# A four-layer vision state-space network in one kernel: layer 1's norms and gate in turns, the sampled convolution in halves, the projection with a bank per tile

## The reference

```python
# layer 0 (sampled convolution)
xz = einsum('bchw,ec->behw', x, in_proj_w); xin, z = split(xz, 2); z = silu(z)
t = gelu(batch_norm(conv3x3(xin, off1_w) + off1_b))
offset = tanh(conv1x1(t, off2_w)) * [1/(H-1), 1/(W-1)]
x_s = grid_sample_bilinear(xin, offset + ref)      # shifts of 0 to 1 point in y and x
# layer 1 (norm over channels, and a gate over the four directions)
xn = (x - mean_c(x)) * rsqrt(var_c(x) + 1e-5) * norm_g + norm_b
gate = softmax(tanh(xn @ gate_w1.T + gate_b1) @ gate_w2.T + gate_b2)
outs = mamba of xn in 4 directions;  y = sum_k gate[k] * outs[k]
```

## Time and profile before

| | us |
|---|---|
| median of 3 runs (lowest, highest) | 30857.21 (30854.06, 30863.32) |
| the profiled execution | 30855.04 |
| its span | 30853.3 |

### The profile page before, as it was taken

One profiled execution on the slowest core, in us unless ns is written; L12 is line 12 of the kernel. 1 busy time (PEld: TensorE's weight loads), 2 busy tenths in 40 slices (PEclk: granted clock), 3 DMA queues, 4 the chain that ended last, 5 costly groups with the idle time before them and its releaser, 6 DMA issues. The chain is left out here.

```text
span 30853.3 us, 332186 instructions
## 1 busy us (share of the span) xinstructions
PE 23829.2 (77%) x97030; PEld 7351.8 (24%) x97030; DVE 25538.5 (83%) x16489; ACT 14890.1 (48%) x20203; POOL 22839.6 (74%) x10221
## 2 busy tenths in 40 slices
PE   6877888888435688888886778888883778888885
PEld 3442222222112222222222422222221422222222
DVE  1259999999535999999993799999994689999995
ACT  1045555555134655555531555555551455555552
POOL 0028999999003699999992299999990189999991
PEclk8888888888756688888876888888886888888887
DMA  2042222221504422222235522222215532222224
GB/s 75 10 164 70 45 45 45 49 50 38 178 9 157 160 52 45 45 45 47 52 110 180 208 61 45 45 50 49 45 38 199 189 86 45 51 48 45 45 45 170
DMA packets 1155007, 2419.20 MB, mean 78 GB/s; under 512 B 118600, under 2 KB 656166, under 8 KB 1143680
## 3 DMA queue, kind: packets, MB, share of 16 engines
q1 hardware_dynamic: 1153224, 2397.86, 28.2%
HBM read 1374.43 MB, written 1023.05 MB: 78 GB/s over the span
## 5 line engine op out<-in xcount | busy, mean ns | idle before, releaser
L1355 POOL TENSOR_TENSOR scan_hc<-scan_bc,scan_h 128x1024 f32<-128x1024 f32 x6912 | 16086.7, 2362 | 108.3 <-DVE scan_h L1519 107.3
L1519 DVE TENSOR_TENSOR_SCAN scan_h<-scan_da,scan_state,scan_dbu 128x1024 f32<-128x1024 f32 x6912 | 15987.4, 2338 | 140.1 <-ACT scan_da L1407 133.9
L1438 PE MATMUL scan_da<-scan_dd,scan_ssel 32*128 32x512 f32 x27648 | 9101.0, 745 | 3013.1 <-DVE scan_h L1519 2781.0
L1407 ACT ACTIVATE scan_da<-scan_da,scan_a_cur 128x1024 f32<-128x1024 f32 x6912 | 7516.7, 1087 | 7720.6 <-PE scan_da L1438 7714.2
L1438 PE MATMUL scan_p_du<-scan_dd,scan_ssel 32*128 32x512 f32 x27648 | 9198.0, 745 | 534.2 <-DMA scan_bc<-bc_d 214.2
L1506 DVE TENSOR_TENSOR scan_dbu<-scan_p_du,scan_bc 128x1024 f32<-128x1024 f32 x4608 | 5561.0, 1207 | 506.1 <-PE scan_p_du L1438 475.5
L1341 POOL TENSOR_TENSOR scan_dbu<-scan_bc,scan_dus 128x1024 f32<-128x1024 f32 x2304 | 5446.0, 2364 | 145.7 <-ACT scan_dus L1381 145.1
L1438 PEld LDWEIGHTS scan_da<-scan_dd,scan_ssel 32*128 32x128 f32 x27648 | 2450.3, 216 | 10296.4 <-DVE scan_h L1519 8730.6
L1455 PE MATMUL scan_p_y<-scan_hc,scan_rsel 128*32 128x512 f32 x27648 | 4778.1, 772 | 17.2 <-POOL scan_hc L1355 16.8
L1438 PEld LDWEIGHTS scan_p_du<-scan_dd,scan_ssel 32*128 32x128 f32 x27648 | 2409.9, 211 | 3617.2 <-DVE scan_dbu L1506 2962.3
L1386 ACT ACTIVATE scan_state<-scan_h,scan_a_cur 128x1 f32<-128x1 f32 x6912 | 2025.1, 293 | 1584.3 <-DVE scan_h L1519 1476.4
(11 more groups left out here) (215 smaller groups left out, 14787.6 us busy)
## 6 DMA issues: line engine op xcount, KB each, us to landing
scan_bc<-bc_d SPq DMA_DIRECT2D x576, 512.0 KB, 12.1
du_d<-prep_useq SPq DMA_DIRECT2D x384, 576.0 KB, 3.8
delta_d<-prep_delta SPq DMA_DIRECT2D x384, 576.0 KB, 4.3
scan_dd<-delta_d SPq DMA_DIRECT2D x1152, 192.0 KB, 4.9
scan_dd<-du_d SPq DMA_DIRECT2D x1152, 192.0 KB, 6.7
y_d<-scan_y SPq DMA_DIRECT2D x576, 384.0 KB, 5.8
merge_y<-y_d SPq DMA_DIRECT2D x384, 576.0 KB, 5.8
xs_d<-proj_xs_o SPq DMA_DIRECT2D x96, 588.0 KB, 3.3
```

What stands on the lines that cost most here:

```text
L1355: nc.gpsimd.tensor_tensor(hc[:, u % HC_SLOTS, :], c, h[:, u % H_SLOTS, :], ALU.mult).then_inc(hc_ready, 1)
L1407: nc.scalar.activation(da[u % DELTA_BANKS][:], da[u % DELTA_BANKS][:], ACT.Exp, scale=a_cur[:, slot(u)[0], u % UNITS:u % UNITS + 1]).then_ ...
L1438: return nc.tensor.matmul(dst[:, half * H:(half + 1) * H], ssel[rows, i, :], dd[rows, s, m, j, :], start=True, stop=True)
L1519: nc.vector.tensor_tensor_scan(h[:, v % H_SLOTS, :], da[v % DELTA_BANKS][:], dbu[:, v % DBU_SLOTS, :], state[:, v % UNITS:v % UNITS + 1], ...
```

## The change

`norm_gate` is written in turns: turn t makes the first stage of step t, the second of step t-1 and so on up to the sixth turn behind, for both images at once. Mean and group scale are folded into one matmul with scaled centring weights (`scaled_c`); the variance is reduced to two rows, one an image, and the reciprocal of its root is spread back with gamma by a matmul; the hidden layers of both images lie in rows 0 to 31 and 32 to 63. Buffers are two or four deep.

`group_norm_head` waits for each half image on its own and loads the averaging weights last. `project` has eight banks, one a tile, copies and activates tile by tile, computes the third tile by two matmuls of 64 columns in place of two accumulating ones of 128, has its x (or `xn`) on 128 rows of which 32 are zeroed by POOL, and in layer 1 reads x in quarters with no copy. `conv_sampled` loads the grid in four bands, uses halves of 64 rows or 64 columns for the blocks that were half zero, and has offsets and spreads of earlier steps between the low part (tiles 0 and 1) and the high part (tile 2) of a step; the offset rows are kept twice, at rows 0 and 32, one for each axis. All loops are written out. Layouts of the weights follow.

The diff, cut (blank lines left out, indented less). `norm_gate`:

```diff
+    def centre_x(s):
+        t_.wait_ge(squared, s * IMAGES + ONE)
...
+        for b in range(IMAGES):
+            nc.tensor.matmul(p_c[:, b, 0:N], scaled_c[:, b, :], x[:, b, s * N:(s + 1) * N], start=True,
+                             stop=True).then_inc(centred, 1)
+    def square_sum(s):
+        t_.wait_ge(squared, (s + 1) * IMAGES + ONE)
+        t_.wait_ge(dev_ready, s + ONE)
+        for b in range(IMAGES):
+            last = nc.tensor.matmul(p_v[:, 0:N], mean[:, b, :], sq[:, s % 2, b, :], start=(b == 0), stop=(b == 1))
+        last.then_inc(var_done, 1)
...
+    def spread(s):
+        t_.wait_ge(inv_ready, s + 1 + ONE)
+        t_.wait_ge(scaled, s + ONE)
+        for b in range(IMAGES):
+            last = nc.tensor.matmul(p_r[:, b, 0:N], gamma[:, b, :], rs[:, s % 2, :], start=True, stop=True)
+        last.then_inc(scale_spread, 1)
+    def hide(s):
+        t_.wait_ge(xl_ready, s + 1 + ONE)
+        t_.wait_ge(tanh_ready, s + ONE)
+        for b in range(IMAGES):
+            q = HID_ROWS[b]
+            last = nc.tensor.matmul(p_hid[q:q + GATE_ROWS, 0:N], w1[:], xl[:, s % DEEP, b, :], start=True, stop=True)
+        last.then_inc(hidden, 1)
...
+    def make_logits(s):
+        t_.wait_ge(tanh_ready, s + 1 + ONE)
+        t_.wait_ge(soft, max((s - 1) * SOFT + 1, 0) + ONE)
+        for m in range(BLOCKS_T):
+            last = nc.tensor.matmul(p_log[:, m * IMAGES:(m + 1) * IMAGES, :].rearrange("p b k -> p (b k)"),
+                                    th[:, s % 2, m * P:(m + 1) * P], w2[:], start=True, stop=True)
+        last.then_inc(logits, 1)
...
+    def transpose(s):
+        t_.wait_ge(soft, (s + 1) * SOFT + ONE)
+        t_.wait_ge(gt_ready, s + ONE)
+        for m in range(BLOCKS_T):
+            last = nc.tensor.transpose(p_gt[:, m * P:(m + 1) * P],
+                                       lg[:, s % DEEP, m * IMAGES:(m + 1) * IMAGES, :].rearrange("p b k -> p (b k)"), eye[:])
+        last.then_inc(transposed, 1)
...
+    for t in range(TURNS):
+        if step(t):
+            centre_x(t)
+        if step(t - 1):
+            square_sum(t - 1)
+        if step(t - 2):
+            spread(t - 2)
+        if step(t - 3):
+            hide(t - 3)
+        if step(t - 4):
+            make_logits(t - 4)
+        if step(t - 6):
+            transpose(t - 6)
...
+    def deviation(s):
+        a.wait_ge(var_done, s + 1 + ONE)
+        a.wait_ge(inv_ready, s + ONE)
+        nc.scalar.activation(sd[:], p_v[:, 0:N], ACT.Sqrt, bias=eps[:]).then_inc(dev_ready, 1)
...
+    def square(s):
+        a.wait_ge(scaled, max(s - DEEP + 1, 0) + ONE)
+        a.wait_ge(var_done, max(s - 1, 0) + ONE)
+        for b in range(IMAGES):
+            a.wait_ge(centred, s * IMAGES + b + 1 + ONE)
+            nc.scalar.activation(xc[:, s % DEEP, b, :], p_c[:, b, 0:N], ACT.Identity, bias=shift[:, b:b + 1]).then_inc(xc_ready, 1)
+            nc.scalar.activation(sq[:, s % 2, b, :], p_c[:, b, 0:N], ACT.Square, bias=shift[:, b:b + 1]).then_inc(squared, 1)
...
+    def add_beta(s):
+        a.wait_ge(scaled, s + 1 + ONE)
+        a.wait_ge(xl_stored[s % DEEP], 16 * (s // DEEP) + ONE)
+        a.wait_ge(hidden, max(s - DEEP + 1, 0) + ONE)
+        nc.scalar.activation(xl[:, s % DEEP], xr[:, s % 2], ACT.Identity, bias=vecs[:, 1:2]).then_inc(xl_ready, 1)
...
+    def hyperbolic(s):
+        a.wait_ge(hidden, s + 1 + ONE)
+        a.wait_ge(logits, max(s - 1, 0) + ONE)
+        nc.scalar.activation(th[:, s % 2, :], p_hid[:, 0:N], ACT.Tanh, bias=b1[:]).then_inc(tanh_ready, 1)
...
+    def exponential(s):
+        a.wait_ge(soft, s * SOFT + 3 + ONE)
+        nc.scalar.activation(lg[:, s % DEEP], lg[:, s % DEEP], ACT.Exp).then_inc(exp_ready, 1)
...
+    for t in range(TURNS):
+        if step(t - 1):
+            deviation(t - 1)
+        if step(t):
+            square(t)
+        if step(t - 2):
+            add_beta(t - 2)
+        if step(t - 3):
+            hyperbolic(t - 3)
+        if step(t - 4):
+            exponential(t - 4)
...
+    def invert(s):
+        d.wait_ge(dev_ready, s + 1 + ONE)
+        d.wait_ge(scale_spread, max(s - 1, 0) + ONE)
+        nc.vector.reciprocal(rs[:, s % 2, :], sd[:]).then_inc(inv_ready, 1)
...
+    def scale_x(s):
+        d.wait_ge(scale_spread, s + 1 + ONE)
+        d.wait_ge(xc_ready, (s + 1) * IMAGES + ONE)
+        d.wait_ge(xl_ready, max(s - 1, 0) + ONE)
+        nc.vector.tensor_tensor(xr[:, s % 2], xc[:, s % DEEP], p_r[:, :, 0:N], ALU.mult).then_inc(scaled, 1)
...
+    def soft_shift(s):
+        own = lg[:, s % DEEP]
+        d.wait_ge(logits, s + 1 + ONE)
+        d.wait_ge(transposed, max(s - DEEP + 1, 0) + ONE)
+        nc.vector.tensor_tensor(own, p_log[:], b2[:].unsqueeze(1).broadcast_to([P, BLOCKS_T * IMAGES, DIRS]), ALU.add).then_inc(soft, 1)
...
+    def take_gates(s):
+        d.wait_ge(transposed, s + 1 + ONE)
+        d.wait_ge(gt_stored[s % DEEP], 16 * (s // DEEP) + ONE)
+        nc.vector.tensor_copy(gt[:, s % DEEP, :], p_gt[:, 0:N]).then_inc(gt_ready, 1)
...
+    for t in range(TURNS):
+        if step(t - 5):
+            soft_divide(t - 5)
+        if step(t - 2):
+            scale_x(t - 2)
+        if step(t - 4):
+            soft_shift(t - 4)
+        if step(t - 1):
+            invert(t - 1)
+        if step(t - 6):
+            take_gates(t - 6)
```

`group_norm_head`:

```diff
-            sp.dma_start(x[:, b, h * L // 2:(h + 1) * L // 2], x_d[b, :, h * L // 2:(h + 1) * L // 2]).then_inc(loaded, 16)
+            sp.dma_start(x[:, b, h * L // 2:(h + 1) * L // 2], x_d[b, :, h * L // 2:(h + 1) * L // 2]).then_inc(half_loaded[2 * b + h], 16)
+    sp.dma_start(avg[:], w["avg"]).then_inc(loaded, 16)
...
         for n in range(NBN):
-            d.wait_ge(loaded, 16 * 5 + ONE)
+            d.wait_ge(half_loaded[2 * b + n // (NBN // 2)], 16 + ONE)
```

`project`:

```diff
+        def bank_of(s, half, m):
+return bank[(s * 2 * TILES + half * TILES + m) % BANKS]
...
+        for n in range(QUARTERS):
+            sp.dma_start(x[0:CH, :, n * q:(n + 1) * q], x_d[:, :, n * q:(n + 1) * q].rearrange("b c n -> c b n")).then_inc(x_in[n], 16)
+    for s in range(STEPS):
...
+    def normalise(s):
+        a.wait_ge(z_psum, max(s - 1, 0) * TILES + ONE)
+        for b in range(IMAGES):
+            nc.scalar.activation(xn[0:CH, s % 2, b, :], x[:, b, s * N:(s + 1) * N], ACT.Identity, bias=bias[:, b:b + 1],
+                                 scale=scale[:, b:b + 1]).then_inc(xn_ready, 1)
+    if not normed:
+        normalise(0)
+    for s in range(STEPS):
+        if not normed and s + 1 < STEPS:
+            normalise(s + 1)
+        a.wait_ge(z_stored[s % DEEP], 16 * (s // DEEP) + ONE)
+        for m in range(TILES):
+            a.wait_ge(z_psum, s * TILES + m + 1 + ONE)
+            nc.scalar.activation(z_o[:, s % DEEP, m, :], bank_of(s, 1, m)[:, 0:N], ACT.Silu).then_inc(z_ready, 1)
...
+    def free(s, half, m):
+        n = s * 2 * TILES + half * TILES + m - BANKS
+        if n >= 0:
+            before, o = divmod(n, 2 * TILES)
+            if o < TILES:
+                t.wait_ge(xs_ready, before * TILES + o + 1 + ONE)
+            else:
+                t.wait_ge(z_ready, before * TILES + o - TILES + 1 + ONE)
...
+        if normed:
+            t.wait_ge(x_in[s * QUARTERS // STEPS], 16 + ONE)
+            src = [x[:, b, s * N:(s + 1) * N] for b in range(IMAGES)]
+        else:
+            t.wait_ge(xn_ready, (s + 1) * IMAGES + ONE)
+            src = [xn[:, s % 2, b, :] for b in range(IMAGES)]
+        for half, done in ((0, xs_psum), (1, z_psum)):
+            for m in range(TILES):
+                free(s, half, m)
+            for b in range(IMAGES):
+                nc.tensor.matmul(bank_of(s, half, b)[:, 0:N], win[:, half, 0, :], src[b], start=True, stop=True).then_inc(done, 1)
+            for b in range(IMAGES):
+                rows = slice(b * HALF, (b + 1) * HALF)
+                last = nc.tensor.matmul(bank_of(s, half, 2)[rows, 0:N], win[:, half, 1 + b, rows], src[b], start=True, stop=True)
+            last.then_inc(done, 1)
 @block.vector
 def _(d):
-    d.wait_ge(zeroed, 1 + ONE)
-    with d.Fori(0, STEPS // 2) as i:
```

`conv_sampled`:

```diff
+        sp.dma_start(grid[:, :, 1 + b * BAND:1 + (b + 1) * BAND, :].rearrange("p t r c -> p t (r c)"),
+                     xs_d[:, :, b * BAND * PADDED:(b + 1) * BAND * PADDED]).then_inc(rows_loaded[b], 16)
+        if b == 0:
+            for dst, src in ((taps, w["taps"]), (bn, w["bn"]), (off_w, w["off_w"]), (off_sel, w["off_sel"])):
+                sp.dma_start(dst[:], src).then_inc(loaded, 16)
+    for s in range(STEPS):
+        sp.wait_ge(lerp, (s + 1) * TILES * STEP + ONE)
...
+    def convolve_low(s):
+        t.wait_ge(rows_loaded[band(s)], 16 + ONE)
+        t.wait_ge(gelu_done, max(s * TILES - 1, 0) + ONE)
+        for tap in range(TAPS):
+            first, end = tap == 0, tap == TAPS - 1
+            for m in range(2):
+                nc.tensor.matmul(p_conv[:, m, 0:N], taps[:, tap, 0, :], rows_of(s, m, tap), start=first, stop=False)
+            for m in range(2):
```

(53 more changed lines are left out.)

522 lines of the change are left out of this document (254 added, 268 removed).

## The result

The changed kernel takes 29109.4 us (median of 4 runs, 29087.84 to 29122.94), the kernel before 30855.64 beside it (4 runs, 30836.15 to 30863.32). The ratio is 0.9434, 95% interval 0.9419 to 0.9449: 1746 us less, where 1743 were forecast. The two profiled executions are 30855.04 and 29087.84 us, 1767 apart; all that follows is read from these two.

The account below looks back on a forecast made before the run. It took the changed stages to be bound by waiting in chains between engines, with no engine full over the span. Savings of 389 + 21 + 480 + 179 + 64 + 620, less 10, gave 29110 us; range 28930 to 29520.

Parts of the forecast that it names:

- The step's price: Sampled convolution: 40.3 us a step, PE-bound, 41.2 at clock 0.95; the loop saves 389 us.
- The load: Sampled convolution: the grid comes in four bands, the first matmul waits only for the first, saving 21 us.
- the sentence that gave halves a small part and order nearly all: Sampled convolution: halving saves only 4 us a step; the large saving is order, other engines working beside matmuls.
- Its 128 rows instead of 96 cost nothing, as a pass goes by its columns: Layer 1's projection: widening to 128 rows adds no matmul time; that projection saves 179 us.
- Rival B: Projection and gate: slow loads or stores add 58 us, a gate at 1.2 GHz adds 120; 29290 us; chance 0.15.
- ACT's 7.4: Norm and gate: ACT's work in a turn is 7.4 us; 8 us a turn was said, saving 620.
- the prediction's sign of being right: Norm and gate: turns of 8 us with ACT busy over 85%.
- The upper bound of the prediction: Norm and gate: with PE at 1.2 GHz a turn takes 13 us, 120 us more.
- The fee of 10 us for more semaphores: Whole kernel: some fifty more semaphores to set and clear cost 10 us, an estimate of 0 to 20.
- A: Convolution and projection: halves do not overlap yet pay the changes of shape, +276 and +123; 29510 us; chance 0.13.
- C: Convolution: drains keep the clock at 1.2 GHz and halves do not overlap; slower than before, 31560 us; chance 0.02.
- D: Gate: in-order queues wait in a ring, a turn stays near 17 us, +216; 29330 us; chance 0.06.

Follow-up runs that it names:

- kernel 3: Changed kernel with the projection's matmuls reading 96 rows instead of 128, zero rows still written: 29484.27 us.
- kernels 1 and 6: Changed kernel with, in 1, the convolution's half blocks computed whole: 29235.41 us; in 6, the convolution's old step order, halves kept: 29282.12 us.
- kernel 4: Changed kernel with the gate's centring, variance and hidden-layer matmuls on 128 rows, 32 of them zero: 29051.25 us.
- kernel 10: Kernel before with only the group norm's heads changed, statistics of each half of x as it lands: 30792.73 us.
- kernels 1 and 2: Changed kernel with, in 1, the convolution's half blocks computed whole: 29235.41 us; in 2, the convolution's matmuls grouped by shape: 28965.77 us.

## Why the prediction was right, and where not

The time was right (29110 for 29109), and the term that is furthest off misses by 32 us of 620. That it came out to 1 us is luck: the terms miss by -32 to +25 and cancel, and the runs of the changed kernel alone lie 35 us apart. And the full clock in the projection hung on 32 rows of zeros to which the prediction gave no part in it (kernel 3).

**Convolution, +25 us.** The step's price stood on four readings, and each held: 0.32 a whole pass, half passes in pairs, 0.19 a change, and PE without a gap. Two sizes were off. The granted clock was 0.99 and not the 0.95 taken from the finishing stage, worth 1.1 us a step, some 26 in all (the prediction adds only 2.5% for 0.95, where 1 / 0.95 would be 5%; at 5% the miss would have been twice that). The load gave 23 us and not 21: the first matmul went from 392.67 to 189.33, 203.3 us earlier, of which 180.1 were gained before. The prediction's own working does not give its 21; 49.6 less the 20 of the first band and taps is 30. What failed is the sentence that gave halves a small part and order nearly all: kernels 1 and 6 give 5.3 and 7.7 us a step, of 18.2.

**Projection, +9 and -5 us.** 4.57 for 4.6 a step. But "Its 128 rows instead of 96 cost nothing, as a pass goes by its columns" saw half of it: they cost nothing and they are worth 375 us (kernel 3). Without them the prediction's own price for a step, made at full clock, would have been wrong by 4.1 us, and no row of the trace before could have said so: there 96 rows got full clock in bursts. Rival B named the clock as the danger, but for the gate only.

**Gate, -32 us: the limit was the wrong one.** The prediction took PE's turn as 6.9 us "at full clock", set ACT's 7.4 as the limit and said 8. At full clock this was about right: kernel 4 shows turns of 6.9, ACT 95% busy; in the changed kernel ACT is at 67% (144.09 of 215.70), where the prediction's sign of being right was over 85%. But PE was granted 0.60 on average in the stage, a turn at the low level is 11.5 us, PE alone, and the mean is 9.4. The upper bound of the prediction, 13 us a turn, covered it (its terms add up to 13.6, so PE at the low clock throughout would have been 134 us more and not 120); of rival B's 120 us, a quarter came. The reason named there, narrow shapes that leave PE waiting, is not it: PE hardly waited (211.62 of 215.70 busy), and kernel 4, which changes only the rows of centring, variance and hidden layer from 96 to 128, brings the high clock.

**Heads, +4, and the rest, +23.** Sixteen us each as worked out, and kernel 10 has them alone. The fee of 10 us for more semaphores did not show. The 13 us came in the unchanged stretch from layer 1's projection to layer 2's head, 7020.9 us before and 7007.8 after; over all twelve profiled executions it took 7008 to 7025, so they are scatter and no effect of the change.

**Rivals.** A (halves do not overlap) is out by kernels 1 and 2. B came true in part in the gate; the stores never limited (DMA share 0.63 in the projection, 0.83 in layer 1's, whose steps are no longer). C (slower: 1.2 GHz through the convolution) did not come, but kernel 3 shows its mechanism alive in the projection: half shapes at the low clock for a whole stage with PE never idle. Its chance of 0.02 was too low for what the trace before could exclude. (Its sum takes off 111 us for heads and loads, where the prediction's own terms are 64 + 21 = 85; C stays slower than before either way.) D is out: in the gate PE waits 4 of 215.7 us.

What stays open: why 96 rows with halves are kept at 1.2 GHz and 128 rows with halves, or 96 with whole passes, are not. The runs give three of the four combinations of rows and halves for the projection, and 96 against 128 rows for the gate; they don't give a rule, and they don't part the half passes from the changes of shape beside them.

## What to carry to other kernels

Price the halves of the PE array as the pair's one slot plus about 0.2 us for each change of shape, and group matmuls by shape: that alone was worth as much again as the halves. When a dense stage's passes of 384 columns are 0.64 us apart and not 0.32 though PE never pauses, try the same matmuls on 128 rows with zeros before looking for a wait. When every engine is below half in a stage, write its steps as turns and read the limit off one turn: PE, ACT and the chain that can't be cut, each at both clock levels.
